# Causal attention in a macaron block: the weighted values move from between score heads 2 and 3 to between score heads 1 and 2

## What is computed

```
x = x + 0.5 * ffn(layernorm(x), gate, up, down)
x = x + attention(layernorm(x), w_project, w_out)
x = x + 0.5 * ffn(layernorm(x), gate, up, down)
```

```
att = einsum('bhqd,bhkd->bhqk', q, k) / sqrt(16)
att = where(causal, -1e9, att)
att = softmax(att)
out = einsum('bhqk,bhkd->bhqd', att, v)
```

## Time and profile before

| what | us |
|---|---|
| median of three runs | 1101.98 (1101.21 to 1102.24) |
| the profiled execution's own time | 1102.49 |
| its span in the trace | 1100.4 |
| TensorE busy | 1028.3 |
| VectorE busy | 716.2 |
| ScalarE busy | 447.6 |
| the 160 steps with their last copy | about 372.7 to 838.6 of the span |

### The profile page before, as it was taken

The page is one execution under the profiler, slowest core; times in us unless marked ns, Lnnn a source line. Parts: engine busy times, 40 slices in busy tenths (PEclk is TensorE's granted clock), DMA queues, the critical chain, the costliest instruction groups (busy, mean ns, idle before and its releaser), DMA issues.

```text
span 1100.4 us, 16127 instructions
## 1 busy us (share of the span) xinstructions
PE 1028.3 (93%) x6214; PEld 472.8 (43%) x6214; DVE 716.2 (65%) x1138; ACT 447.6 (41%) x859; POOL 111.3 (10%) x140
## 2 busy tenths in 40 slices
PE   3789999999988589999999999999999999999998
PEld 2346545454555244433333323333324454544544
DVE  6975473736547488888887888888803836546362
ACT  2223120202133356565577666677795202112120
POOL 4647110100051000100000000000000100001000
PEclk9889999999999799999999999999999999999999
DMA  7000000000039401000020000000000000000000
GB/s 236 1 0 2 1 1 1 0 0 1 1 71 158 89 11 25 9 1 2 1 31 1 1 1 1 2 1 1 1 1 1 1 1 20 1 19 0 20 1 20
DMA packets 22060, 20.19 MB, mean 18 GB/s; under 512 B 4328, under 2 KB 21736, under 8 KB 21992
## 3 DMA queue, kind: packets, MB, share of 16 engines
q1 hardware_dynamic: 18792, 16.13, 7.5%
q10 hardware_dynamic: 3200, 3.15, 0.9%
HBM read 12.78 MB, written 6.29 MB: 17 GB/s over the span
## 4 chain that ended last, share of the span: by engine, by line
PE 82%; DVE 10%; DMA 4%; issue 1%; POOL 1%; ACT 1%; SPq 1%; DVEq 0%; ACTq 0%; POOLq 0%
PE ps L1081 12%; PE ps L970 10%; PE ps L1045 10%; PE ps L1067 10%; PE ps L934 10%; PE ps L936 10%; PE ps L935 10%; PE ps L971 5%; DVE m_part L846 4%; DMA qk_split<-wreg 3%; PE ps L1054 2%; DVE oT L631 1%; PE ps L928 1%; PE ps L1013 1%; PE ps L919 1%
## 5 line engine op out<-in xcount | busy, mean ns | idle before, releaser
L566 ACT ACTIVATE wreg<-ps 128x512 f32<-128x512 f32 (+3 forms) x640 | 303.9, 536 | 153.0 <-PE ps L1067 78.0
L846 DVE TENSOR_REDUCE m_part<-ps 128x1 f32<-128x1024 f32 (+7 forms) x320 | 326.6, 1060 | 57.1 <-PE ps L1054 28.7
L521 ACT ACTIVATE wreg<-ps,gelu_in 128x512 f32<-128x512 f32 x128 | 88.2, 689 | 357.9 <-PE ps L936 357.9
L1067 PE MATMUL ps<-qreg,kreg 128*128 128x512 f16 (+3 forms) x640 | 181.0, 351 | 14.7 <-DMA qreg<-m_rows 13.0
L718 DVE SCALAR_TENSOR_TENSOR wreg<-ps,kappa,wreg 128x512 f32<-128x512 f32 x128 | 96.0, 750 | 147.0 <-PE ps L936 147.0
L1045 PE MATMUL ps<-kreg,qreg 128*128 128x512 f16 (+3 forms) x640 | 174.8, 350 | 7.8 <-DVE m_part L846 5.6
L970 PE MATMUL ps<-wd,qreg 128*128 128x512 f16 x512 | 166.8, 379 | 0.0
L1081 PE MATMUL ps<-wreg,v 128*17 128x512 f32 (+3 forms) x1280 | 149.8, 534 | 0.8 <-ACT oT L493 0.8
L971 PE MATMUL ps<-wd,qreg 128*128 128x256 f16 x512 | 139.6, 273 | 0.0
L1067 PEld LDWEIGHTS ps<-qreg,kreg 128*128 128x128 f16 x640 | 58.9, 97 | 135.4 <-ACT wreg L566 91.5
L934 PE MATMUL ps<-xT,wg 128*128 128x512 f16 x256 | 98.7, 386 | 2.4 <-issue 2.4
(11 more groups left out here) (133 smaller groups left out, 929.3 us busy)
## 6 DMA issues: line engine op xcount, KB each, us to landing
qk_split<-wreg SPq DMA_DIRECT2D x4, 1024.0 KB, 10.2
kreg<-qk_split SPq DMA_DIRECT2D x24, 128.0 KB, 4.2
qreg<-qk_split SPq DMA_DIRECT2D x24, 128.0 KB, 8.8
xres<-in_L_attn_x ACTq DMA_DIRECT2D x4, 512.0 KB, 8.5
out_x<-xres SPq DMA_DIRECT2D x4, 512.0 KB, 3.0
kreg<-in_L_ffn_up_W_packed ACTq DMA_DIRECT2D x4, 256.0 KB, 6.8
kreg<-in_L_ffn_gate_W_packed SPq DMA_DIRECT2D x4, 256.0 KB, 7.3
kreg<-in_L_ffn_down_W_packed SPq DMA_DIRECT2D x1, 1024.0 KB, 9.7
```

Source lines behind the costliest of these rows:

```text
L521: act.activation(gelu_ring[:, n % 3, :], bank(n % 2), ACT.Gelu_apprx_tanh, scale=gelu_in[:, 0:1]).then_inc(s_gelu, 1)
L566: act.activation(wreg[:, b % 8, 0:CT - q0], bank(score_bank[b], CT - q0), ACT.Exp, scale=EXP_SCALE).then_inc(s_p, 1)
L846: dve.tensor_reduce(m_part[:, r, part, col:col + 8 * (cnt - 1) + 1:8], src, AX.X, ALU.max)\
L1067: last = pe.matmul(dst, kreg[:, pair, P * j:P * j + P], qreg[:, c % 2, h % 2, pair, q0:CT], start=True, stop=not diag)
```

## The change

```diff
--- before.py
+++ after.py
@@ -1121,7 +1121,7 @@
                 parts = [lambda: (scores(t, 0), scores(t, 1)), lambda: scores(t, 2), lambda: scores(t, 3)]
                 if t:
-                    parts.insert(2, lambda: weighted_values(t - 1))
+                    parts.insert(1, lambda: weighted_values(t - 1))
                 for k, part in enumerate(parts):
                     part()
                     for u in plan[t][len(plan[t]) * k // len(parts):len(plan[t]) * (k + 1) // len(parts)]:
```

## The result

The changed kernel takes 1132.96 us (median of four runs, 1130.23 to 1135.72) against 1102.10 us before (four runs, 1101.21 to 1102.24): 30.9 us more, a ratio of 1.028 with a 95% interval of 1.026 to 1.031. The profiled execution took 1132.28 us, its span is 1130.2 us, 29.8 more than before.

The account below looks back on a forecast made before the run. The prediction took TensorE's in-order stream to set the end. Its terms, 4.3 + 6.5 + 12.4 + 2.7 + 6.4 + 0.5 + 1.5, summed to 34.3 us more, giving a median of 1136 us, range 1118 to 1149.

Parts of the forecast that it names:

- Late head 3: Weighted values on TensorE: a late exponential of head 3 is not hidden by other heads, moving the end one for one.
- (a): Ordinary full two-unit steps: weighted values wait 0.14 us for the exponential of score 3; 31 steps, 4.3 us.
- (b): First steps of groups: weighted values wait about 0.65 us for ScalarE's copy behind exponential 3; 6.5 us in all.
- (e): Last group, without units as cover: period 2.54 us against 2.04, waiting for exponential 3; 6.4 us in all.
- (c): Three-unit steps: units with one score between neighbours stall TensorE on VectorE's maxima; 12.4 us, bounds 3 to 17.
- The rival that bursts are absorbed: Only waits on exponentials count, VectorE catching up on crowded units within the same step; 1122 us, chance 0.18.
- (d): Steps with an empty place, around "negate" and "rows", and 140 to 143: +1.5, -1.5 and +2.7, sum 2.7 us.
- (g): Steps with "o", "split", "project": crowded work ahead of VectorE can cost something in ten of them; 1.5 us (0 to 5).
- The clock: Rival: new stalls every 3 us make TensorE's clock fall, two stretches adding some 7 us each; 1150 us, chance 0.06.
- The rival "faster": A late head's passes overlap the others' and cost nothing, while bank waits and waits ahead of "rows" go; 1096 us, chance 0.04.

Follow-up runs that it names:

- Experiment 1: Kernel before, with the weighted values moved one score earlier in the last group's sixteen steps alone; 1107.76 us against 1102.64.
- Experiment 2: Kernel before, with the weighted values ahead of all four scores in the last group alone; 1123.60 us, ratio 1.018.
- Experiment 7: Changed kernel, with exponentials over 256 instead of 512 columns in the last group's full steps; 1128.91 us, ratio 1.025.
- Experiment 5: Changed kernel, with ScalarE's copy of the finished group behind exponential 1 instead of 3 of the next group's first step; 1131.35 us, ratio 1.027.
- Experiment 3: Changed kernel, but units keep their old side of the weighted values, so only score 2 changes sides; 1111.77 us against 1102.64.
- Experiment 6: Changed kernel, with units put back on their old side of the weighted values only in steps with three or more units; 1123.29 us, ratio 1.020.
- Experiment 4: Kernel before, with the weighted values moved the other way, behind score 3 of the next step, in all groups; 1107.59 us, ratio 1.004.
- experiments 5 to 8: Experiment 8, not named singly: kernel before, weighted values behind head 3 in the last twenty steps, last group's copy behind exponential 2; 1100.91 us against 1102.02.

## Why the prediction was right

Forecast 1136, range 1118 to 1149, measured 1132.96. Direction, mechanism and most prices held.

- **Late head 3 is paid in full.** Right, and the statement on which (a), (b) and (e) stood, half of the sum. Experiments 1, 2 and 7 give periods of 2.53, 3.51 and 2.11 us for 2.54, 3.52 and 2.09 worked out before they ran. The spacing of 0.49 us in these sums is right by luck of a slip: (1.62 - 0.63)/2 takes off the length of the copy instead of an exponential's 0.60, which would give 0.51; four exponentials of the changed kernel give (2.06 - 0.60)/3 = 0.49.
- **(a)** 0.14 us a step was right (2.82 to 2.96 us), but I charged it to all 31 steps; 20 of them paid it, those whose unit streams mask products on top of 1024 columns 0.03 to 0.09, and two beside a VectorE wait nothing: 3.4 for 4.3.
- **(b)** 0.65 us was right for eight of the nine plain first steps (2.82 to 3.47 in chunk 2; 0.62 once the shifted units are subtracted in chunk 3); step 24, which took 3.53 us before, paid nothing. For the others I took too much: 5.7 for 6.5. The wait for the copy shows in ten groups, not in nearly all. Experiment 5 shows the copy's place in ScalarE's order as the cause of more than half.
- **(c)** The period of 3.84 us was right (3.88 in steps with units of 1024), and the eleven steps that stand alone pay 0.52 us each for 0.55. Too large was the number of other steps that pay: where TensorE was already waiting for VectorE, the new stall could replace an old one (step 42 went from 4.69 to 4.58 us, no change at all once the units that left it are subtracted), and three of the narrow ones pay 0.15 for 0.25. 10.8 for 12.4. The rival that bursts are absorbed is out by experiments 3 and 6.
- **(d)** 1.7 for 2.7. Waits ahead of "rows" went from 3.2 us in the earlier trace rows to 3.9; the forecast's two terms for them, -1.5 and +2.7, come to +1.2.
- **(g)** The step that was mis-sized the other way: 3.3 for 1.5. The same burst acts on "o", "split" and "project", which now wait for maxima too (4.2 us in L1013, L1017 and L1021 behind L846, 0.2 before). I had allowed 0 to 5.
- **The clock** stayed at 1.00 through the steps, with stalls of 0.3 to 1.0 us every few microseconds. The rival is out here. What the Trainium skill tells in "TensorE: Matmul & The Clock Gate", A second HAM failure mode, of short idle times that bring the clock down, these runs do not show.
- **The rival "faster"** needed a late head that costs nothing; the earlier trace rows had spoken against it, and the last group confirms it.

Experiment 4 corrects a picture that the prediction left open, that more distance behind the last score can only help. It fails at the banks and at the units.

## What to carry to other kernels

When a block is moved in a hand-written order, count three distances and not one: from the last producer to the block, between the other things that the block used to hold apart (here units with two slots), and between buffers reused in turn. A block of several heads in parallel waits for its latest head in full, and the loss stands inside its records, so the busy share stays high. Where a queue in order feeds the block, each score moved away costs the distance of one more exponential ahead of the last (0.49 us here), not its own 0.22.

## What was not expected

- Runs of one kernel lie some 5 us apart: the changed one 1130.23 to 1135.72, the one before 1101.21 to 1102.24 in the first comparison and 1099.69 to 1104.50 in the 15 runs beside experiments 5 to 8. The cause stays open; the wait for a DMA ahead of step 0, which differs by 3.2 us between the two profiles, is a candidate that was not tried.
- Putting the copy earlier saved 0.5 us in each plain first step of chunk 2 and 0.25 in those of chunk 3, where 0.3 was expected for all. Behind it the late head 3 sets the end again, and in chunk 3 the bank of exponential 2 delays the stream as well.
- Half of the new loss, 15.2 us, stands in the profile as busy time of TensorE; 11.8 of it is in the records of L1081.
